# Second cross attention behind its selection: gate folded into weights, spectrum multiplied from PSUM, norms placed beside products

## The reference, cut to what matters

```
scale_in, shift_in = split(c_t @ W_film_in + b_film_in)
x = layernorm(x_text) * g_norm_in + b_norm_in
x = x * (1 + mod_gate * scale_in) + mod_gate * shift_in
y = irfft(rfft(x) * Kf) + x * D_skip
scale_out, shift_out = split(c_t @ W_film_out + b_film_out)
y = y * (1 + mod_gate * scale_out) + mod_gate * shift_out
xt = x_text + y
h = layernorm(xt) * g_ffn + b_ffn
h = gelu(h @ W1 + b1) @ W2 + b2
out = layernorm(xt + h) * g_norm_out + b_norm_out      # and x = x + out
```

## Time and profile before

| what | us |
|---|---|
| median of 3 runs | 2346.48 |
| lowest and highest | 2339.76, 2350.98 |
| profiled execution | 2345.02 |
| its span | 2343.2 |

### The profile page before, as it was taken

The page is one execution under the profiler, slowest core; times in us unless marked ns, Lnnn a source line. Parts: engine busy times, 40 slices in busy tenths (PEclk is TensorE's granted clock), DMA queues, the critical chain, the costliest instruction groups (busy, mean ns, idle before and its releaser), DMA issues.

```text
span 2343.2 us, 34857 instructions
## 1 busy us (share of the span) xinstructions
PE 1861.1 (79%) x13676; PEld 1136.0 (48%) x13676; DVE 1253.5 (53%) x3081; ACT 1029.8 (44%) x1381; POOL 769.4 (33%) x685
## 2 busy tenths in 40 slices
PE   5879999999999988886878687876877376766775
PEld 2434544454454445654664244544544355454553
DVE  5143332424233103556764859979789934636575
ACT  1357567657766871122212435455455211013452
POOL 6244334414432300001200457857678221310000
PEclk7989999999999999998886556777777698778887
DMA  6656557555553600002000011312211340000000
GB/s 139 126 102 117 114 117 120 119 116 107 114 118 88 114 39 1 2 2 92 27 2 12 14 55 48 88 50 60 82 48 55 106 152 1 0 1 1 1 5 14
DMA packets 78046, 150.27 MB, mean 64 GB/s; under 512 B 15464, under 2 KB 63144, under 8 KB 71464
## 3 DMA queue, kind: packets, MB, share of 16 engines
q1 hardware_dynamic: 64304, 102.06, 15.5%
q0 software_dynamic: 12768, 42.59, 11.8%
q10 hardware_dynamic: 792, 3.17, 0.3%
HBM read 93.85 MB, written 2.62 MB: 41 GB/s over the span
## 4 chain that ended last, share of the span: by engine, by line
PE 51%; DVE 25%; ACT 12%; issue 6%; DMA 4%; POOL 3%; DVEq 0%; ACTq 0%; POOLq 0%; SPq 0%
PE R L112 32%; PE B L112 17%; ACT P L571 6%; DVE PM L1700 6%; DVE CA L1658 4%; POOL KST L789 2%; DMA KST<-OV 2%; ACT PM L1585 2%; PE B L178 2%; DVE CA L1670 1%; DVE T L1672 1%; ACT PS L2253 1%; DVE RT L604 1%; DMA CT<-in_ctxT 1%; ACT RT L116 1%
## 5 line engine op out<-in xcount | busy, mean ns | idle before, releaser
L571 ACT ACTIVATE P<-R 128x1024 f32<-128x1024 f32 x512 | 506.9, 1026 | 217.6 <-PE R L112 182.6
L112 PE MATMUL R<-QS,KST 100*128 100x256 bf16 x2048 | 295.5, 276 | 61.8 <-ACT P L571 54.2
L112 PEld LDWEIGHTS R<-QS,KST 100*128 100x128 bf16 x2048 | 169.2, 98 | 225.5 <-ACT P L571 121.8
L116 ACT ACTIVATE SC<-R 128x1024 f32<-128x1024 f32 x128 | 129.6, 1024 | 240.3 <-PE R L112 129.5
L1658 DVE MAX8 CA<-SC 128x8 f32<-128x128 f32 x1024 | 203.2, 277 | 15.7 <-ACT SC L116 14.8
L200 POOL TENSOR_TENSOR LNrs<-LNve,pk_const 128x2 f32<-128x2 f32 x36 | 25.4, 705 | 521.5 <-DVE LNve L196 521.4
L112 PE MATMUL R<-OV,QT 32*128 32x512 f32 x512 | 190.9, 834 | 0.0
L1773 POOL TENSOR_TENSOR ACC<-ACC,PM 128x4096 f32<-128x4096 f32 x21 | 186.2, 8867 | 1.7
L1700 DVE SCALAR_TENSOR_TENSOR PM<-SC,T,PM 128x4096 f32<-128x4096 f32 x32 | 149.7, 4713 | 41.0 <-ACT AT L116 21.0
L789 POOL DMA_DIRECT2D KST<-OV x300 | 145.1, 492 | 73.8 <-PE R L112 56.4
L112 PE MATMUL R<-P,VP 128*32 128x256 f32 x2304 | 154.8, 385 | 1.0 <-ACT P L571 1.0
(11 more groups left out here) (364 smaller groups left out, 3407.3 us busy)
## 6 DMA issues: line engine op xcount, KB each, us to landing
KST<-OV POOLq DMA_DIRECT2D x276, 128.0 KB, 10.8
CT<-in_ctxP SPq DMA_DIRECT2D x40, 768.0 KB, 4.4
CN<-in_ctxn SPq DMA_DIRECT2D x64, 384.0 KB, 3.4
CT<-in_ctxT SPq DMA_DIRECT2D x64, 192.0 KB, 2.4
KST<-OV SPq DMA_DIRECT2D x84, 128.0 KB, 10.9
KST<-in_ctxP ACTq DMA_DIRECT2D x4, 768.0 KB, 9.1
QS<-x_q POOLq DMA_DIRECT2D x24, 128.0 KB, 5.5
pk_a<-in_pk_a SPq DMA_DIRECT2D x1, 3014.0 KB, 17.8
```

The lines of the kernel that those rows point to most:

```text
L112: return e.matmul(o, l, r, start=st, stop=sp, skip_group_check=True)
L116: return e.activation(o, i, ACT.Copy)
L571: e.activation(P[(32 * p + k0) % 3][:, :], ring.at(("s", p, k0))[:, :], ACT.Exp).then_inc(*EX.up((p, k0)))
```

## The change

The change stays within stage_x1b, apart from the pack x1c, in which gf and bf are no longer repeated over 128 partitions but stored by column (gfc, bfc).

- The gate is multiplied into the film weights and biases once, at the stage's start, on VectorE (six instructions), with the 1 of "1 + scale" added to the bias; GpSimd's scalings go. The first film products wait for it.
- VectorE multiplies the spectrum straight from PSUM by the real and by the imaginary half of KF, 1024 elements at a time (XR, XI), then two sums of 512; ScalarE's copy XF and GpSimd's product go. u times D_skip moves from GpSimd to VectorE.
- Gain and bias of the third norm are applied by ScalarE in the copy to HT; ScalarE therefore waits for x1c at the start of the stage.
- The bias b2 moves from VectorE to GpSimd, beside the feed-forward, with bo.
- On VectorE the first two norms of batches 2 and 3 run at steps 9 and 10 of the pair before; steps 6 and 7 are one step, and so are 12 and 13; gi and bi come before the film addition.
- ScalarE's first copy of batches 2 and 3 waits for products of two batches back, and its second for the inverse transform's use of CT2, instead of for the residual.

The diff, cut to its core:

```diff
@@ tensor
+                        if b == 0:
+                            e.wait_ge(*V.at("gated " + nm))
...
-                        ps, free = ring.take(("xf", b), (S, ("xf", b)))
+                        ps, free = ring.take(("xf", b), (V, ("xs", b)))
...
-                        e.wait_ge(*V.at(("hb", b)))
+                        e.wait_ge(*V.at(("hn", b)))
@@ scalar
+                e.wait_ge(*LC1.at("x1c"))
...
                         if b >= 2:
-                            e.wait_ge(*V.at(("x", b - 2)))
+                            e.wait_ge(*M.at(("c2", b - 2)))
...
+                        if b >= 2:
+                            e.wait_ge(*V.at(("y", b - 2)))
                         e.wait_ge(*M.at(("c2", b)))
...
-                    elif s == 4:
-                        e.wait_ge(*M.at(("xf", b)))
-                        acopy(e, XF, two(ring.at(("xf", b))[:, :], 4)).then_inc(*S.up(("xf", b)))
...
-                        acopy(e, HT, two(bank.at(("ht", b))[:, :])).then_inc(*S.up(("ht", b)))
+                        for k in range(2):
+                            ins = e.activation(HT[:, k, :], two(bank.at(("ht", b))[:, :])[:, k, :], ACT.Identity, bias=w["bfc"][:, k:k + 1], scale=w["gfc"][:, k:k + 1])
+                        ins.then_inc(*S.up(("ht", b)))
@@ vector
+                e.wait_ge(*LB.at("x1b"))
+                for nm in ("fin", "fout"):
+                    e.tensor_scalar(w[nm], w[nm], w["mg"], None, ALU.mult).then_inc(*V.up("gated " + nm))
+                    bias = w[nm + "b"]
+                    e.tensor_scalar(bias[:, 0:256], bias[:, 0:256], w["mg"], 1.0, ALU.mult, ALU.add).then_inc(*V.up())
+                    e.tensor_scalar(bias[:, 256:512], bias[:, 256:512], w["mg"], None, ALU.mult).then_inc(*V.up())
...
-                        e.tensor_tensor(YF[:, re, :], XF[:, re, :], KF[:, re, :], ALU.mult).then_inc(*V.up())
-                        e.tensor_tensor(TA, XF[:, im, :], KF[:, im, :], ALU.mult).then_inc(*V.up())
-                        e.tensor_tensor(XQ, XF[:, im, :], KF[:, re, :], ALU.mult).then_inc(*V.up())
-                        link(YF[:, re, :], YF[:, re, :], TA, ALU.subtract)
-                        e.wait_ge(*G.at(("yi", b)))
-                        link(YF[:, im, :], YF[:, im, :], XQ, ALU.add, ("yf", b))
+                        xf = two(ring.at(("xf", b))[:, :])
+                        e.wait_ge(*M.at(("xf", b)))
+                        e.tensor_tensor(XR, xf, kre, ALU.mult).then_inc(*V.up())
+                        e.tensor_tensor(XI, xf, kim, ALU.mult).then_inc(*V.up(("xs", b)))
+                        yf = YF.rearrange("p (h a) n -> p h (a n)", h=2)
+                        link(yf[:, 0, :], XR[:, 0, :], XI[:, 1, :], ALU.subtract)
+                        e.tensor_tensor(yf[:, 1, :], XR[:, 1, :], XI[:, 0, :], ALU.add).then_inc(*V.up(("yf", b)))
...
+                    elif s == 9 and b + 2 < NB:
+                        first_norm(b + 2)
+                    elif s == 10 and b + 2 < NB:
+                        second_norm(b + 2)
@@ gpsimd
+                    elif s == 8:
+                        e.wait_ge(*V.at(("hn", b | 1)))
+                        e.tensor_tensor(XQ, XQ, row2(w["b2"]), ALU.add).then_inc(*G.up(("b2", b)))
                         e.tensor_tensor(xrows(b), xrows(b), row2(w["bo"]), ALU.add).then_inc(*G.up(("xb", b)))
```

More of the change, by code:

```diff
@@ L1900, in tensor @@
                             e.wait_ge(*S.at(("ht", b)))
-                            e.wait_ge(*LC1.at("x1c"))
                         for f in range(4):
@@ L1949, in link, with first_norm, second_norm @@
                     e.tensor_tensor(o, x, y, op).then_inc(*V.up(key))
+                def first_norm(b):
+                    norm_stats(e, b % 2, xrows(b), V, ("ve0", b))
+                    e.wait_ge(*G.at(("rs0", b)))
+                    norm_apply(e, b % 2, xrows(b), nb["XN", b % 2], V, ("xn", b))
+                def second_norm(b):
+                    e.wait_ge(*V.at(("xn", b)))
+                    norm_stats(e, b % 2, nb["XN", b % 2], V, ("ve1", b))
+                    e.wait_ge(*G.at(("rs1", b)))
+                    norm_apply(e, b % 2, nb["XN", b % 2], nb["u", b % 2], V, ("un", b))
@@ L1952, in vector @@
                 e.tensor_copy(KF[:, :, :], two(ring.at("kf")[:, :], 4)).then_inc(*V.up("kf"))
+                kre, kim = (row2(KF[:, 2 * h:2 * h + 2, :].rearrange("p a n -> p (a n)"), 512) for h in range(2))
                 for b, s in order:
                     i = b % 2
-                    XN, FI, FO, u, CT2, XF, YF, TA, XQ, HN = (nb[nm, i] for nm in ("XN", "FI", "FO", "u", "CT2", "XF", "YF", "TA", "XQ", "HN"))
+                    XN, FI, FO, u, CT2, XR, XI, YF, XQ, HN = (nb[nm, i] for nm in ("XN", "FI", "FO", "u", "CT2", "XR", "XI", "YF", "XQ", "HN"))
@@ L1956, in vector @@
                     xb = xrows(b)
[L1957 to L1970 removed]
+                    if s == 0 and b < 2:
+                        first_norm(b)
+                    elif s == 1 and b < 2:
+                        second_norm(b)
+                    elif s == 2:
@@ L1994, in vector @@
                         link(XQ, u, XN, ALU.add, ("xq", b))
-                    elif s == 7:
                         e.wait_ge(*V.at(("xq", b)))
@@ L2628, in host_layout @@
                         mg=bcast(x1["mod_gate"].reshape(1)), F=rows(Fm, 128), Gi=rows(Gm, 128))
-    packs["x1c"] = dict(bi=bcast(x1["b_norm_in"]), go=bcast(x1["g_norm_out"]), bo=bcast(x1["b_norm_out"]), gf=bcast(x1["g_ffn"]),
-                        bf=bcast(x1["b_ffn"]), Dsk=bcast(x1["D_skip"]), b2=bcast(x1["b2"]), b1=x1["b1"].reshape(8, 128).T,
+    packs["x1c"] = dict(bi=bcast(x1["b_norm_in"]), go=bcast(x1["g_norm_out"]), bo=bcast(x1["b_norm_out"]), gfc=x1["g_ffn"].reshape(2, 128).T,
+                        bfc=x1["b_ffn"].reshape(2, 128).T, Dsk=bcast(x1["D_skip"]), b2=bcast(x1["b2"]), b1=x1["b1"].reshape(8, 128).T,
                         W1=rows(x1["W1"], 128), W2=rows(x1["W2"], 128))
```

67 lines of the change are left out of this document (24 added, 43 removed).

## The result

The changed kernel took 2307.24 us as the median of four executions (2303.67 to 2318.84), the kernel before beside it 2343.99; the ratio is 0.985, with a 95% interval of 0.981 to 0.989. A second set of four executions of the changed kernel, taken later, gave 2304.57 against 2345.98, ratio 0.982 (0.980 to 0.984).

A forecast was written before the change was run, and what follows sets the result against it. No engine is always busy, so the changed stage's chain of waits (205 of 2343 us) counts. First pair -6.6, handover -7.0, second pair -22.4, end -4.0: together -40.0 us, giving a median of 2306; range 2296 to 2320.

The forecast's parts named there:

- first copy waits for the pack: Stage start: ScalarE's first copy, now waiting for pack x1c to land, comes 6.0 us late.
- half clock up to film's end: First pair: after TensorE's pause at the start, copy to end of film takes 24.1 us against 19.7, +4.4.
- transposes to last product, first pair: First pair, second batch's transposes through feed-forward: the 30.3 us stay as they were.
- handover: Between first pair's last product and second pair's first copy: ScalarE waits for products, not the residual; -7.0 us.
- film at full clock, second pair: Second pair's film: TensorE pauses under 1 us before it and keeps its clock; -4.4 us.
- end of the stage: After the last product: only the second batch's last steps remain, 4.8 to 5.0 us; -4.0 us.
- The start: Stage start up to film's end, first pair: late first copy +6.0 us, then half clock +4.4 us.
- The upper bound of this wait: Stage start: ScalarE's copy waits until the next pack lands, at 17.8 us, 7.4 us more.
- The gate: Stage start: six added vector operations, at most 4.5 us, 3.8 in idle time; nothing on the path.
- Film to transforms: Each pair: first transform follows film without pause, -4.9 us, and runs at full clock, -2.4 and -3.0 us.
- transform to transposes: Each pair, first transform's end to second batch's transposes: vector work alone, 18.9 us; -9.7 and -10.1 us.
- The hidden part: Beside feed-forward: GpSimd's bias additions and next pair's norms, 17.6 us, fit with 5.7 us cover; rival of failure 0.05.

The follow-up runs named there:

- Experiment one: Changed kernel with ScalarE's wait for the pack x1c moved from the stage's start to its first copy with gain; 2295.08 us, ratio 0.980, stage 155.5 us.
- the experiment with the copy: Changed kernel with ScalarE's copy of the spectrum to SBUF back and VectorE's two multiplications reading it; stage 165.5 us against 165.7 and 163.7.
- the kernel with GpSimd's product: Changed kernel with ScalarE's spectrum copy back and half of VectorE's second multiplication (512 elements) given to GpSimd; stage 172.4 us.

## Why the prediction was right

It said 2306 us; 2307.24 was measured, and 2304.57 in the second set. Its terms, against the profiled execution (all as after less before, in us):

| term | predicted | measured |
|---|---|---|
| first copy waits for the pack | +6.0 | 10.29 - 4.25 = +6.0 |
| half clock up to film's end | +4.4 | 24.2 - 19.6 = +4.6 |
| film to the first transform's end, first pair | -7.3 | 3.45 - 10.8 = -7.3 |
| first transform to transposes, first pair | -9.7 | 19.0 - 28.6 = -9.6 |
| transposes to last product, first pair | 0 | 30.9 - 30.3 = +0.6 |
| handover | -7.0 | 0.5 - 7.5 = -7.0 |
| film at full clock, second pair | -4.4 | 19.7 - 24.1 = -4.4 |
| film to the first transform's end, second pair | -7.9 | 3.45 - 11.35 = -7.9 |
| first transform to transposes, second pair | -10.1 | 19.05 - 28.95 = -9.9 |
| transposes to last product, second pair | 0 | 29.95 - 30.4 = -0.4 |
| end of the stage | -4.0 | 5.2 - 9.0 = -3.8 |
| sum | -40.0 | -39.1 |

As far as the timeline shows, the mechanism was right in all terms but one, the handover. That both medians came within 1.5 us of the forecast is luck on top of it: single executions of the changed kernel lie up to 17 us apart. Its two profiled ones differ by 12.5 us, 8.2 of them in the selection stage, and in the second the first two terms were 5.2 and 4.0. Point by point:

- *The start.* The 0.8 us taken off for the smaller pack came out as 0.9 (it landed 10.07 us after the issue). Experiment one shows both terms to be real and avoidable: together 10.3 us against the first profile of the changed kernel and 8.2 against the second, where the prediction's two terms together are 10.4. One premise was read wrongly: TensorE's pause at the start was said to be longer than that of the handover, but by the prediction's own times it is under 7 us (measured 6.8), where the handover's was 7.8. The clock was lost all the same. The upper bound of this wait was 7.4 us more; by the issue of the next pack at 1894.83 and its 17.8 us it is 8.0.
- *The gate.* Nothing on the path was right for its cost, but the part alone gains at least 0.7 us per pair through GpSimd's silence, a gain that the prediction did not name. In the whole change it is covered, since that stretch is gone.
- *Film to transforms* and *transform to transposes* went by the rows to 0.2 us. That PSUM costs VectorE no more than SBUF is shown by the experiment with the copy, and so is the copy's price, 1.05 us per pair. The advice that the prediction set against the edit (the Trainium skill, "VectorE: DVE Perf Modes", Rules for kernel authors) would have cost here what the rows said, about 1 us per pair.
- *The handover* had the right size, but the cause given for it is not the one that the change needs. The step that failed is "ScalarE's copy waited for the residual of two batches back (7.5 us); now it waits for products only". With that wait back, the third batch's copy is where it was. The gain comes from VectorE's order, in which the first batch's residual no longer stands behind the second batch's norm. Whether the new wait would have given it in the old order is open.
- *The hidden part* was hidden with room: GpSimd's four additions ran from 1967.58 to 1972.5, so 1.26 us each and not 1.7, and the norms were done 9.6 us before VectorE's next work.
- *The range* was needed less for the stage than for what lies outside it. The profiled execution was 13 us above the forecast although its stage was within 1 us of it.

## What to carry to other kernels

Look at what a moved weight does to the first wait of a stage: a constant that one copy needs late was waited for at the stage's start, and this one line cost 8 to 10 us of a gain of about 49, nearly half of it in clock. Where two batches are woven step by step, finish the first batch's last step before starting the second's, and put work that needs no new data (here the next pair's norms) beside long products; a wait that looks guilty may be harmless once the order is right. A pause of TensorE that can't be removed can be split by products that nobody reads, if a free PSUM slot is at hand: here two pauses of 5 us, split in this way, gave 4.6 us of the stage.

## What the runs showed of the hardware

- The clock's recovery varies between executions. From the first copy to film's end, after pauses of 5.9 to 7.6 us, it took 21.6 to 25.1 us in eight profiled executions with the same products there, against 19.6 without the pause, so stage lengths differ by up to 3.5 us by this alone. The shortest of the eight followed the longest pause.
- A pause of 3.09 us of TensorE, with the same work around it, was followed by half clock in the first pair and by full clock in the second (the kernel with GpSimd's product, 0.53 and 1.00).
- The selection stage, whose code no experiment touched, took one of three lengths over the 13 profiled executions, from its first copy of scores to the first product behind it: 635.7 to 636.1 us five times (the kernel before is one of them), 639.5 to 640.0 three times, and 645.9 to 648.0 five times (the changed kernel's first profile among them; its second took 639.5). The mean granted clock over 1264 to 1880 us was 0.68 in the first group, 0.67 in the second and 0.66 to 0.67 in the last. Why it falls into groups was not tried.
- VectorE's scale of 1024 fp32 elements within SBUF took 0.75 us, where the copy of as many from PSUM took 1.23.
- GpSimd's additions took 1.26 us beside VectorE's norms. Its product took 2.31 where VectorE's multiplication had begun before it and 1.26 where it began first; then VectorE's instruction took the longer time, 1.76 us against 0.69.
